# ViT tower with a state-space mixer and routed experts: second normalisation through centred weights and squares, two small steps moved to other engines, and the order of work written anew

## What is computed

```python
h = concat(cls_tok, patches(x) @ W.T + b)                 # 64 images x 197 tokens x 192
a = layernorm(h)
x_inner, z = split(a @ W_in)                              # 384 channels each
x_conv = silu(conv4(x_inner) + conv_b)
B, C   = split(x_conv @ W_x)                              # 16 states each
delta  = softplus(x_conv @ W_dt + b_dt)
# per token, channel, state:  h_s = exp(delta * A) * h_s + delta * x_conv * B
y   = sum_s(h_s * C) + D * x_conv
out = (y * silu(z)) @ W_out
h   = h + (out - mean) * rsqrt(var + 1e-5) * gamma + beta # "second normalisation"
h   = h + switch_ffn(layernorm(h))                        # 8 experts, capacity limit
```

## Time and profile before

| | us |
|---|---|
| median of 3 runs | 3194.55 (3191.55 to 3195.04) |
| the profiled execution | 3200.91 |
| its span, first to last instruction | 3199.2 |
| pipeline from the first `bx` (125.45) to the end of the last scan (2474.3) | 2348.9 |
| drain of the pipeline and router, to about | 2696 |
| expert stage, to the end | 503 |

### The profile page before, as it was taken

How to read it: one execution, slowest core, us unless ns; L and a number is a source line. 1 busy time by engine, 2 the same in 40 slices (tenths; PEclk the granted TensorE clock), 3 DMA queues, 4 the chain that set the end, 5 groups by cost and what they waited for, 6 DMA issues and landing times.

```text
span 3199.2 us, 38052 instructions
## 1 busy us (share of the span) xinstructions
PE 2576.5 (81%) x12731; PEld 1591.3 (50%) x12731; DVE 2519.0 (79%) x2798; ACT 1902.9 (59%) x3691; POOL 2264.1 (71%) x1412
## 2 busy tenths in 40 slices
PE   5688887888888888877888888888875464999998
PEld 3344444444444444444444444444432353888887
DVE  1499999999999999999999999999999644222222
ACT  0577677776777777776777777777764001433433
POOL 0377788887878787887888878888877692444443
PEclk8889898888999899998899999999986676999999
DMA  2334444554544444444555444444442101666663
GB/s 92 91 92 99 99 114 114 115 125 107 116 100 99 99 99 99 99 118 109 116 120 117 112 99 99 99 99 99 114 96 64 72 1 39 219 210 210 212 213 116
DMA packets 165465, 361.09 MB, mean 113 GB/s; under 512 B 18353, under 2 KB 89593, under 8 KB 157848
## 3 DMA queue, kind: packets, MB, share of 16 engines
q1 hardware_dynamic: 152504, 329.59, 41.0%
q0 software_dynamic: 12768, 29.08, 2.7%
HBM read 293.86 MB, written 69.30 MB: 114 GB/s over the span
## 4 chain that ended last, share of the span: by engine, by line
PE 38%; DVE 32%; issue 13%; ACT 11%; POOL 4%; DMA 1%; SPq 0%; DVEq 0%; POOLq 0%; ACTq 0%
DVE arena L1280 14%; DVE arena L1271 11%; PE banks L1191 7%; PE banks L1175 5%; PE banks L925 4%; PE banks L888 4%; POOL arena L612 3%; PE banks L1180 3%; PE banks L954 2%; PE banks L916 2%; PE banks L907 2%; ACT banks L662 2%; ACT arena L669 1%; DVE arena L1309 1%; DVE arena L1254 1%
## 5 line engine op out<-in xcount | busy, mean ns | idle before, releaser
L485 POOL TENSOR_TENSOR arena<-arena 128x1576 f32<-128x1576 f32 x384 | 1245.0, 3258 | 285.6 <-DVE arena L1280 285.6
L1280 DVE TENSOR_TENSOR_SCAN arena<-banks,arena 128x788 f32<-128x788 f32 x768 | 1359.6, 1789 | 58.1 <-ACT banks L662 19.9
L662 ACT ACTIVATE banks<-arena,neg_a 128x392 f32<-128x392 f32 x1536 | 842.2, 581 | 420.3 <-DVE arena L1280 411.2
L1271 DVE TENSOR_TENSOR arena<-arena,banks 128x1576 f32<-128x1576 f32 x384 | 681.0, 1773 | 30.3 <-DMA arena<-delta_du_scratch 19.6
L954 PE MATMUL banks<-arena,gather_q 128*32 128x394 f32 x3072 | 379.0, 569 | 0.3 <-POOL arena L485 0.3
L1521 DVE TENSOR_TENSOR arena<-banks,arena 128x384 f32<-128x384 f32 x57 | 31.8, 557 | 384.1 <-PE banks L1191 384.1
L630 POOL DMA_INDIRECT out_tokens<-arena x114 | 115.2, 1011 | 280.5 <-DVE arena L1527 263.1
L888 PE MATMUL banks<-wtok,arena 128*99 128x192 f32 x1536 | 264.5, 330 | 49.1 <-ACT arena L729 44.3
L907 PE MATMUL banks<-arena,v_lo 128*128 128x394 f32 x768 | 291.7, 523 | 2.8 <-DVE logits L1303 1.3
L888 PEld LDWEIGHTS banks<-wtok,arena 128*99 128x99 f32 x1536 | 249.2, 167 | 81.2 <-ACT arena L729 65.6
L669 ACT ACTIVATE arena<-arena 99x192 f32<-99x192 f32 x384 | 178.8, 536 | 125.8 <-POOL arena L479 121.7
(11 more groups left out here) (210 smaller groups left out, 4306.2 us busy)
## 6 DMA issues: line engine op xcount, KB each, us to landing
arena<-delta_du_scratch SPq DMA_DIRECT2D x384, 394.0 KB, 11.2
arena<-in_w_pack SPq DMA_DIRECT2D x57, 1155.0 KB
delta_du_scratch<-arena SPq DMA_DIRECT2D x96, 394.0 KB, 3.2
arena<-in_x SPq DMA_DIRECT2D x32, 1176.0 KB, 15.5
rows_scratch<-arena SPq DMA_DIRECT2D x32, 297.0 KB
rows_scratch<-arena SPq DMA_DIRECT2D x32, 294.0 KB
arena<-in_b SPq DMA_DIRECT2D x57, 96.0 KB
arena<-in_conv_w SPq DMA_DIRECT2D x1, 2304.0 KB, 9.2
```

Source lines behind the costliest of these rows:

```text
L485: pool.tensor_tensor(v[:, :, :], v[:, :, :], c_rep[r][:, u % NG].unsqueeze(1).to_broadcast([P, NQ, N2]), ALU.mult).then_inc(s_mulp, 1)
L662: ins = act.activation(o, d, ACT.Exp, scale=neg_a[:, c:c + 1])
L1271: dve.tensor_tensor(hb[u % BUFS][:, :, :], rep[m][:, :, 1, :], ps_b[:, 0:N2].unsqueeze(1).to_broadcast([P, NQ, N2]), ALU.mult).then_inc(s_ ...
L1280: dve.tensor_tensor_scan(v, decay[k % 2], v, 0.0, ALU.mult, ALU.add).then_inc(s_scan, 1)
```

## The change

1. `W_out` is centred on chip at the start: each row's mean over the 192 outputs is subtracted (three DVE instructions), so `y @ W_out` has mean zero and `out_stats` on DVE goes away. The variance comes from `out_squares` on ACT: four Square activations of 99x192 with the sum in `accum_out`. `rstd_out` on POOL is shorter, and `out_norm` only scales.
2. `last_bc` moves from DVE (32 partitions) to POOL (128 partitions, into `bcf`), and a new ACT copy `third_bc` writes the third part to `bc3`.
3. `softplus_t` moves from DVE to ACT as two activations, `softplus_up` (+1) and the new `softplus_t` (-1).
4. The order of all queues in `body` is written anew. For ACT the steps that matter are listed in the diff; `silu_z` goes from step 9 to step 3, away from `silu_x`, and `row_stats` on DVE from step 20 to step 18.

```diff
+            def rstd_out(n):
+                need(pool, s_onorm, n)
+                pool.wait_ge(s_sq2, n + 1)
+                pool.tensor_scalar(var2[:, :], sq2[:, :], 1.0 / DIM, EPS, ALU.mult, ALU.add).then_inc(s_var2, 1)
+                pool.wait_ge(s_var2, n + 1)
+                pool.tensor_tensor(rs2[:, :], var2[:, :], small[0:H0, 0, :], ALU.pow).then_inc(s_rs2, 1)
+            def last_bc(n, r):
+                pool.wait_ge(s_bcmid, n + 1)
+                pool.tensor_tensor(bcf, bcf, bc3[r], ALU.subtract).then_inc(s_bclast, 1)
...
 # POOL body; in a unit u, in this order
+                    if 0 in on and u == 3: fill_rows(i, r)
+                    if -1 in on and u == 5: rstd_out(i - 1)
                     if 1 in on and u == 6: rest_bc(i + 1, o)
+                    if 1 in on and u == 7: softplus_sum(i + 1)          # was 8
                     if 1 in on and u == 8: make_du(i + 1, o)
+                    if -1 in on and u == 8: add_residual(i - 1, o)
                     if 2 in on and u == 8: rstd(i + 2, 1)
                     if -1 in on and u == 9: rstd(i - 1, 3)
                     if 0 in on and u > 0: times_c(i, r, u - 1)
+                    if -1 in on and u == 5: apply_gamma(i - 1)          # was 8
+                    if 1 in on and u == 7: last_bc(i + 1, o)
+                    if 1 in on and u == 7: softplus_rest(i + 1)         # was 8
+                    if 1 in on and u == 7: make_delta(i + 1)            # was 8
...
+            def out_squares(n, r):
+                act.wait_ge(s_oev, 2 * (n + 1))
...
+                for c in range(4):
+                    ins = act.activation(rows[r][:, c, DIM:2 * DIM], ob[:, c, :], ACT.Square, accum_out=sq2[:, c:c + 1])
+                ins.then_inc(s_sq2, 1)
             def out_norm(n):
-                normalise(n, lambda c: ob[:, c, :], lambda c: ob[:, c, :], rs2, nb2, s_rs2, s_onorm, range(4))
+                act.wait_ge(s_rs2, n + 1)
+                for c in range(4):
+                    ins = act.activation(ob[:, c, :], ob[:, c, :], ACT.Copy, scale=rs2[:, c:c + 1])
+                ins.then_inc(s_onorm, 1)
+            def third_bc(n, r):
+                act.wait_ge(s_bclast, n + 1)
+                act.activation(bc3[r][P - 2 * NS:P], bcf[P - 2 * NS:P], ACT.Copy).then_inc(s_bc3, 1)
+            def softplus_up(n):
+                act.wait_ge(s_spe, n + 1)
+                need(act, s_ddu, DDU * n)
+                act.activation(delta[:, :, :], spe[:, :, :], ACT.Identity, bias=1.0).then_inc(s_spu, 1)
+            def softplus_t(n):
+                act.wait_ge(s_spu, n + 1)
+                act.activation(delta[:, :, :], delta[:, :, :], ACT.Identity, bias=-1.0).then_inc(s_spt, 1)
...
 # ACT body after: what follows decays(i, k) in step k
+ k 0: copy_c 3            k 3: silu_z             k 4, 5, 7: conv copies 0, 1, 2
+ k 8: copy_out 0, and router_exp(FIRST, 1) when i == PAIRS (was i == PAIRS - 1, k 23)
+ k 9: silu_x, copy_out 1, out_squares
+ k 10: copy of B and C    k 11: out_norm, delta product 0    k 12: delta product 1
+ k 13: middle_bc, delta product 2, softplus_exp
+ k 14: softplus_up, softplus_t
+ k 16: third_bc, softplus_ln
+ k 18: copy_c 0           k 19: z 0, z 2, copy_c 1, front_norm
+ k 20: copy_front_t 0, z 1      k 21: copy_c 2, row_norm
+ k 22: copy_back_t 0, 1   k 23: copy_front_t 1
...
 # PE body, units 2 to 5 (after spread_b(u+1) and state_sum of each unit)
+ u 2: conv 2, out_product 0     u 3: out_product 1, bc     u 4: dt 0, dt 1     u 5: dt 2
...
 # DVE
+            dve.tensor_reduce(w_sum, wout[:, :, :], AX.X, ALU.add).then_inc(s_wc0, 1)
+            dve.tensor_scalar(w_sum, w_sum, -1.0 / DIM, None, ALU.mult).then_inc(s_wc0, 1)
+            dve.tensor_tensor(wout[:, :, :], wout[:, :, :], w_sum.unsqueeze(2).to_broadcast([P, MB, DIM]), ALU.add).then_inc(s_wc, 1)
...
-                dve.tensor_tensor(bc3[r][v], bcf[v], bc3[r][v], ALU.subtract).then_inc(s_bc3, 1)
-                stats(n, lambda c: ob[:, c, :], st2, mv2, s_oev, 2 * (n + 1), s_rs2, s_st2, s_mv2)
-                dve.tensor_scalar(delta[:, :, :], spe[:, :, :], 1.0, -1.0, ALU.add, ALU.add).then_inc(s_spt, 1)
+ k 1: take_logits (was 2)   k 4: take_y 2 (was 6)   k 14: take_y 0, embed 0 (was 15)   k 16: embed 1
+ k 17: front_stats          k 18: row_stats (was 20)     k 20: take_y 1 (was 22)
```

More of the change, by code:

```diff
@@ L284, in build @@
         s_spt = sem("softplus_rounded")
+        s_spu = sem("softplus_one_more")
         s_spc = sem("softplus_rest")
@@ L588, in body @@
                             router_consts()
-                    if 0 in on and u == 5:
-                        fill_rows(i, r)
-                    if -1 in on and u == 8:
+                    if -1 in on and u == 5:
                         apply_gamma(i - 1)
-                    if -1 in on and u == 8:
-                        add_residual(i - 1, o)
+                    if 1 in on and u == 7:
+                        last_bc(i + 1, o)
+                    if 1 in on and u == 7:
+                        softplus_rest(i + 1)
+                    if 1 in on and u == 7:
+                        make_delta(i + 1)
             pool.wait_ge(s_pool0, POOL0)
@@ L771, in body @@
                         copy_c(i, r, o, 3)
+                    if 0 in on and k == 3:
+                        silu_z(i, r)
+                    if 1 in on and k == 4:
+                        copy_product(i + 1, o, r, 0)
                     if 1 in on and k == 5:
-                        copy_product(i + 1, o, r, 0)
+                        copy_product(i + 1, o, r, 1)
                     if 1 in on and k == 7:
                         copy_product(i + 1, o, r, 2)
[L776 to L779, removed]
+                    if -1 in on and k == 8:
+                        copy_out(i - 1, r, 0)
+                        if i == PAIRS:
+                            router_exp(FIRST, 1)
                     if 1 in on and k == 9:
@@ L782, in body @@
                     if -1 in on and k == 9:
-                        copy_out(i - 1, r, 0)
-                    if -1 in on and k == 10:
                         copy_out(i - 1, r, 1)
+                    if -1 in on and k == 9:
+                        out_squares(i - 1, o)
+                    if 1 in on and k == 10:
+                        copy_product(i + 1, o, r, BC)
+                    if -1 in on and k == 11:
+                        out_norm(i - 1)
                     if 1 in on and k == 11:
@@ L806, in body @@
-                    if 1 in on and k == 18:
+                    if 1 in on and k == 14:
+                        softplus_up(i + 1)
+                    if 1 in on and k == 14:
+                        softplus_t(i + 1)
+                    if 1 in on and k == 16:
+                        third_bc(i + 1, o)
+                    if 1 in on and k == 16:
+                        softplus_ln(i + 1)
+                    if 1 in on and k == 18:
+                        copy_c(i + 1, o, r, 0)
+                    if 1 in on and k == 19:
+                        copy_product(i + 1, o, r, Z)
@@ L1374, in body @@
                         scan(i, k)
-                    if -2 in on and k == 2:
+                    if -2 in on and k == 1:
                         take_logits(i - 2, o)
@@ L1382, in body @@
                             weigh(FIRST, 1)
-                    if -1 in on and k == 10:
-                        out_stats(i - 1)
                         if i == PAIRS:
@@ L1388, in body @@
                         take_y(i, r, 0)
-                    if 1 in on and k == 15:
-                        last_bc(i + 1, o)
-                    if 1 in on and k == 15:
-                        softplus_t(i + 1)
-                    if 2 in on and k == 15:
+                    if 2 in on and k == 14:
                         embed(i + 2, r, r, 0)
```

182 lines of the change are left out of this document (91 added, 91 removed).

## The result

The changed kernel takes 3205.09 us (median of 6 runs, 3202.11 to 3206.95); the kernel before, run beside it, 3194.53 (3190.50 to 3198.11). The ratio is 1.0034 [1.0022, 1.0047]: **0.34% slower**, where 3189 and more likely faster was forecast.

What follows compares the result with a forecast made beforehand. DVE bound the kernel before; after, ACT from `decays` 9 to scan 17: bare DVE 68.9 plus 4.3 waiting, 73.2 us per iteration. Terms sum to -5.5: 3195.4 against the profiled 3200.91, 3189 on the median's scale, range 3157 to 3222.

Steps and rivals of the forecast that it cites:

- The rival that it might not come: ACT's stretch without `third_bc`'s wait for `last_bc`: 1.2 us shorter; with cheaper squares 3159 us, joint chance 0.20.
- 3233 by the page's price: Steps 3 and 4: at 2.66 us per table switch `decays` 4 comes 1.5 us late, 3189 + 29 x 1.5.
- the step on covers: `bc` ahead of `spread_b` 5 on PE: `bx` 5 1.0 us late, covered by scan 10 waiting for ACT until 1.3.
- a sign of being wrong: Profile after: a wait for PE's spread (or the rep DMA) ahead of `bx` would show the prediction wrong.
- Last pair: Last pair, no front work on ACT: DVE saving 1.5 and a PE wait of 1.1 gone, -2.6 us.
- The loop's term: Iterations between the ends: 29 x 0.03 = +0.9 us, and iteration 30, without embeds to shorten, +1.0.
- the drain: Drain: `row_stats` at step 18 lets `times_c` start two scans earlier; -4.0 us, all the router behind with it.
- the first pair: First pair: ACT is shorter without back-half work, -2.0 us.
- the fill: Pipeline fill: `last_bc` between `softplus_sum` and `softplus_rest` on POOL, hidden by nothing, +1.2 us.
- The dear squares: Rival: ACT's four squares take 3.1 us, putting 1.3 on every iteration; 3228 us, chance 0.12.
- late rep: Rival: `make_du` 1.5 us later than worked out, first `decays` and `bx` wait 1.0 for DMA; 3219, chance 0.05.
- uncovered loads: Rival: the two new table loads at steps 3 and 4 find no cover, 29 x 2.6 = 75; 3264, chance 0.03.

Runs made afterwards that it cites:

- the edit of POOL's order: Changed kernel with `last_bc` ahead of `softplus_sum` and `times_c` on POOL instead of behind them: 3159.53 us, 0.9888 of the kernel before.
- filler run: Changed kernel with 21 matmuls of unused result per iteration, in units 8 and 9 of PE: 3232.22 us, 1.0127 of the kernel before.

## Why the prediction was wrong

**Right: what bounds the loop.** ACT, not DVE, sets the end from `decays` 9 to scan 17. The floor is 73.03 for 73.2 forecast, although DVE has 99 us less to do. Two edits show it: each us taken from ACT's stretch, the wait of `third_bc` or three Squares, came off the floor. ACT's timeline after, against the earlier trace rows:

```profile
1260.89 0.36 ACT L709 ACTIVATE arena<-arena 99x192 f32<-99x192 f32 x1
1261.16 0.19 ACT L709 ACTIVATION_READ_ACCUMULATOR arena<-arena 99x1 f32 x1
1261.26 0.34 ACT L709 ACTIVATE arena<-arena 99x192 f32<-99x192 f32 x1
...
1262.40 1.28 ACT L681 ACT_TABLE_LOAD   x1
1263.70 1.10 ACT L681 ACTIVATE banks<-arena,neg_a 128x392 f32<-128x392 f32 x2
...
1275.72 1.17 ACT L786 ACTIVATE arena<-arena 128x1182 f32<-128x1182 f32 x1
1276.93 1.19 ACT L790 ACTIVATE arena<-arena 128x1182 f32<-128x1182 f32 x1
1278.02 2.11 ACT L681 ACTIVATE banks<-arena,neg_a 128x392 f32<-128x392 f32 x4
1281.28 0.53 ACT L769 ACTIVATE arena<-arena 32x394 bf16<-32x394 f32 x1 [1.16 <-POOL arena L508]
```

- Squares: 1262.40 - 1260.89 = 1.51 for 1.8 taken, inside 1.0 to 3.1. Each writes its sum with an instruction of its own, and the two overlap.
- `softplus_up` and `softplus_t`: 1278.02 - 1275.72 = 2.30, as taken.
- The wait of `third_bc`: 1.16 for 1.2. The rival that it might not come is refuted, and the edit of POOL's order shows that it costs its full length.
- The table loads at step 3 are covered: at none of scans 3 to 5 does DVE wait for ACT. From the load at 1262.40 to the `decays` it is 1.30, as in the earlier trace rows; the Trainium skill ("ScalarE: Activation LUTs", *What ACT_TABLE_LOAD costs*) has 2.66 for a switch, about 1380 ns of it drain (the prediction wrote 1383), which none of the four switches between 1256.88 and 1287 shows. The prediction's 3233 by the page's price is a slip as well: 2 x (2.66 - 1.30) less 1.1 of room is an estimate of 1.6 an iteration and not 1.5.
- `bx` 5 waits 0.93 for 1.0 forecast; it took the place of the wait at scan 10, as the step on covers had it. The last paragraph of the prediction calls a wait for PE's spread ahead of `bx` a sign of being wrong; that contradicts this step, and the sign came although the step was right.
- Last pair: -2.1 for -2.6.

**Wrong: "`spread_c`, `tok` and `front_t` on PE come 0.5 us or more before they are asked for".** That sentence stood for all of PE's hand-overs in the new order, and the third `take_y`, moved two steps towards its `state_sum`, had no term at all. The loop's term, 29 x 0.03 = +0.9 and +1.0 for iteration 30, measured +8.0 and +10.7. With PE at full clock it does have 1322.55 - (1321.06 + 0.87) = 0.6 us to spare, and the floor iterations show no wait. With PE late at the low clock it waits up to 2.26. The forecast took one iteration at full clock for all 31. It is the step that decides the sign: with that `take_y` a step later the kernel takes 3188 us, for 3189 forecast. That the two agree to 1 us is luck, for the other misses are of both signs: the floor 0.17 lower (4.9 us in 29 iterations), the drain 3 and the first pair 2 short of their gain, and 15.5 us above the floor still there, for 13.4 in the profile that the sum was made against.

**Wrong: the drain, -4.0.** It is -0.8. What was forecast did come: the last `take_y` starts 2483.83 - (2477.07 + 1.77) = 5.0 after the last scan, and 2483.23 - 2474.30 = 8.9 in the earlier trace rows, as the earlier `times_c` had it. Right behind it `weigh` stood 5.71 for the router's exponential, which the new order had put behind `copy_out`. The step that failed is "and all of the router behind it with it", which looked only at POOL's queue.

**Wrong: the first pair (-2.0); unresolved: the fill (+1.2).** The first pair came out between -0.5 and +0.3. The forecast counted ACT's work alone; DVE's timeline has waits for PE of 2.59 ahead of `bx` 5 and 1.33 ahead of `take_y` 1 there, for 0.78 and 1.60 ahead of two `bx` before. The fill is lost in its spread.

**The rivals.** None named PE's sums. The dear squares, late rep and uncovered loads, which gave the time the sign it has, are all refuted by the rows above.

**Left open.** What decides in which iterations the clock is low, and why the new order has more of them. The filler run shows that the wait follows the place of the low stretch, not what sets it. Nor is it explained why the kernel before has its median near 3193 on some chips and at 3203 on another; against the latter the changed kernel is not measurably slower, so the 0.34% is a statement on the first of the two chips on which the two kernels ran side by side. The changed kernel itself repeated to 1.1 us (3205.09 and 3203.96).

## What to carry to other kernels

When an order is written anew, list each hand-over in both directions for each moved step, with its slack at the low clock of PE and not only in the one iteration read: a slack of 0.6 us at 2.4 GHz was a wait of 2.3 at 1.2 GHz. Look at several iterations and take the floor and the excess over it apart; a busy share can fall by 99 us and the floor by 0.15. A queue order that is harmless in the loop is read again in the drain, where an instruction with its data ready may stand behind one that waits for the last product.

## What was not expected of the hardware

- An ACT activation with a summed output shows as two instructions, ACTIVATE and ACTIVATION_READ_ACCUMULATOR (187 ns mean over 128), but a pair of 99x192 costs its queue only 0.34 to 0.45 us from start to start.
- Unused matmuls kept PE's granted clock at 1.00 for 33 us, and the next 12 had a mean share of 0.57, most of it at the low level, where it cost some 2 us an iteration.
- Two profiled executions of the kernel before differ by 10.5 us, and only 1.9 of it is in the loop.
